# Turning normalised tokens in two 64-row halves of TensorE's array, each half of the tokens into its own PSUM bank

## The chip, the cores and the metric

The kernel runs on one core of one Trainium2 chip. The metric is the device time of one launch in microseconds. "Before" was timed in three runs; one more execution was profiled. TensorE (PE in the profile) multiplies out of SBUF into PSUM, which has eight banks of 512 fp32 per partition. VectorE is DVE, ScalarE is ACT, GpSimd is POOL, SyncE is SP and issues most DMAs.

## What is computed

One transformer block on a sequence of 4096 tokens of width 256, all in fp32: causal attention over normalised tokens, then a gated feed-forward part. Only the first lines of the attention matter here:

```python
mu = jnp.mean(x, axis=-1, keepdims=True)
var = jnp.mean(jnp.square(x - mu), axis=-1, keepdims=True)
xn = (x - mu) * jax.lax.rsqrt(var + LN_EPS) * gamma + beta
qkv = jnp.einsum('bne,fe->bnf', xn, w_qkv)
...
x = _layernorm(x + _L0_attn_ref(x, L0_attn_gamma, L0_attn_beta, L0_attn_w_qkv), axis=-1)
x = _layernorm(x + _L0_ffn_ref(x, ...), axis=-1)
```

The projection sums over the 256 features, so TensorE needs the features on partitions, while the statistics of a token are taken with tokens on partitions. Each chunk of normalised tokens is therefore turned once, and gamma and beta are applied on the way, where they are one number a partition.

## The kernel before

The tokens are cut in eight chunks of 512 (QB), each four tiles (TI) of 128 tokens. For a chunk c, VectorE takes mean and variance, ScalarE the root and VectorE the reciprocal. Then `normalise(c)` writes `xn_of(c)`, four tiles [128 tokens, 256 features] (VectorE for chunks 0 to 2, L806; POOL for 3 to 7, L609). `transpose_xn(c)` (L998) has TensorE turn them: for each half f of the features it takes one PSUM bank and makes four transposes of 128 tokens by 128 features (L1003), one beside the other, so that bank f holds [128 features, 512 tokens]. `copy_xnt(c)` (L679) has ScalarE copy each bank to `xnT` in one instruction of 512 columns with gamma as scale and beta as bias (L682). Everything that is projected (queries, keys, values) reads `xnT`.

The attention is made of a stream of operations that the class `Schedule` lays out once, in `PLAN.ops`; each engine walks through the same list and does its part. The kinds that matter: `norm` (turn and copy a chunk), `direct` (the first two blocks' queries and keys, L1024, copied by ScalarE in L674 and L676 and summed by POOL in L618), `qk` and `v` (projections, L1015 and L1040), `unit` (a 128-row tile of products whose row maxima VectorE takes, L1054 and L822/L825; for some of them ScalarE first copies one of the two banks to `mx_sb`, L711, and VectorE reduces that, L817), `score` (L1089 and L1094, two banks each; ScalarE takes the exponent in L728), `av` (product with the values, L1111), and `turn` (L1067 and L1075: turned sums and turned maxima, copied by ScalarE in L718 and L744). `norm` 0, 1 and 2 stand in the opening, `norm` 3 to 7 in the loop over blocks, each between the units of one step and an `av`.

Seven of the eight banks form a ring, `ring_bank(use)`. Which bank a use gets is planned by `take_banks`: it walks over the list with a small table of durations in nanoseconds (for a `norm`, 440 of TensorE and 730 of ScalarE for each bank) and gives each use the bank that its model has free first. `former[use]` is the use that had the bank before, and `ring_free(use)` makes TensorE wait for the engine that empties it. So these numbers do not move any instruction, but decide which bank an instruction writes and whom it waits for. Before, `ring_free` was called for bank f just ahead of its four transposes.

Engines signal by semaphores: `xn_done` (normalised tiles), `xnt_ready` (banks turned, one count per bank), `xnt_done` (copies made). TensorE waits for `xnt_done` ahead of the projections of that chunk. ScalarE works through its list strictly in order.

## Time and profile before

| | us |
|---|---|
| median of three runs | 2284.06 |
| lowest and highest run | 2283.5 and 2284.6 |
| profiled execution, its own time | 2284.38 |
| its span in the profile | 2282.8 |
| attention up to about | 1630 |
| feed-forward part from there to the end | 653 |

The page of a profile gives busy times of each engine over the span. PE is the matmul side of TensorE, PEld its weight loads. A timeline merges neighbouring instructions of one form into one row: its start, the length of the whole row, the engine, the line, the tiles and the count; in brackets stands how long the engine was idle ahead of it and who ended that. A group row gives the count, the busy time and the mean length of one, and the idle time ahead of such instructions. The granted TensorE clock is a share of full speed, 1.00 for 2.4 GHz and 0.50 for 1.2 GHz.

### The profile page before, as it was taken

To read this page: it belongs to the slowest core of one execution; us is meant where nothing else is said; L and a number is where in the kernel's file an instruction comes from. 1 tells how busy PE (TensorE), PEld (TensorE's weight loads), DVE (VectorE), ACT (ScalarE), POOL (GpSimd) and SP (SyncE) were. 2 spreads that over 40 slices of the span, in tenths; PEclk is the share of its full clock that TensorE was granted. 3 is DMA by queue.
4 is the path that set the end of the run, shared out by engine and by line. 5 is a ranking of instruction groups with operands and counts; after the bars stand their busy time and mean duration, and the time that the engine had idled before them with its cause. 6 is when DMAs were issued, how large, how long until landed. Compare 5 with 4: busy or idle time off the path is not lost. (4 is left out here: it accounts for less than half of the span.)

```text
span 2282.8 us, 40909 instructions
## 1 busy us (share of the span) xinstructions
PE 2253.1 (99%) x15594; PEld 1394.5 (61%) x15594; DVE 1738.5 (76%) x3748; ACT 1621.0 (71%) x3131; POOL 201.5 (9%) x237
## 2 busy tenths in 40 slices
PE   8999999999999999999999999999999999999998
PEld 5555555555555556555555555554588888888887
DVE  8899998888889897888989898996435445544543
ACT  4677888889999888889989899999723333432332
POOL 3211100011000102000010201001100000000000
PEclk9999999999999999999999999999999999999999
DMA  3110001100000200000020000205410000000000
GB/s 102 31 27 16 5 20 40 38 20 20 20 19 1 59 20 20 20 20 19 1 56 20 20 20 20 77 1 168 151 42 15 5 19 19 10 10 19 15 5 20
DMA packets 72295, 70.22 MB, mean 31 GB/s; under 512 B 41632, under 2 KB 51744, under 8 KB 70688
## 3 DMA queue, kind: packets, MB, share of 16 engines
q1 hardware_dynamic: 67392, 56.03, 9.3%
q0 software_dynamic: 4704, 11.53, 1.7%
q8 instruction: 124, 2.03, 0.4%
q14 instruction: 75, 0.61, 0.1%
HBM read 28.20 MB, written 4.19 MB: 14 GB/s over the span
## 5 line engine op out<-in xcount | busy, mean ns | idle before, releaser
L728 ACT ACTIVATE PR<-bank 128x512 f32<-128x512 f32 (+1 forms) x2176 | 1097.2, 593 | 75.6 <-PE bank L1094 70.6
L822 DVE TENSOR_REDUCE pm<-bank 128x1 f32<-128x512 f32 x1442 | 932.5, 684 | 134.2 <-PE bank L1054 114.9
L1111 PE MATMUL bank<-PR,V 128*17 128x512 f32 (+3 forms) x4608 | 553.2, 562 | 0.3 <-POOL PR L624 0.3
L1089 PE MATMUL bank<-MR,ones 64*128 64x512 f32 (+3 forms) x2304 | 464.7, 383 | 7.1 <-ACT sums L744 4.6
L1499 PE MATMUL bank<-e_hid,e_h_sb 128*128 128x512 f32 x2048 | 466.1, 389 | 0.0
L1499 PEld LDWEIGHTS bank<-e_hid,e_h_sb 128*128 128x128 f32 x2048 | 383.8, 188 | 81.1 <-DVE e_hid L1369 1.5
L1321 ACT ACTIVATE e_tmp<-bank,scales 128x512 f32<-128x512 f32 x128 | 88.3, 690 | 322.8 <-PE bank L1499 322.7
L1089 PEld LDWEIGHTS bank<-MR,ones 64*128 64x128 f32 x2304 | 239.6, 185 | 81.9 <-ACT PR L728 37.1
L825 DVE CUSTOM_DVE_ANT_0 bank<-bank,below 128x256 f32<-128x256 f32 (+3 forms) x512 | 239.9, 514 | 32.0 <-PE bank L1054 30.9
L711 ACT ACTIVATE mx_sb<-bank 128x512 f32<-128x512 f32 x350 | 209.8, 599 | 56.0 <-PE bank L1054 52.1
L1054 PEld LDWEIGHTS bank<-KA,QX 64*128 64x128 f32 x992 | 127.7, 183 | 186.7 <-ACT PR L728 76.9
L1054 PE MATMUL bank<-KA,QX 64*128 64x512 f32 (+3 forms) x992 | 237.5, 438 | 1.6 <-DVE pm L825 0.5
L817 DVE TENSOR_REDUCE pm<-mx_sb 128x1 f32<-128x512 f32 x350 | 236.8, 677 | 0.6
L1448 DVE CAST e_hid<-e_tmp 128x512 fp32r<-128x512 f32 x128 | 54.1, 423 | 237.4 <-ACT e_tmp L1321 237.4
L1094 PE MATMUL bank<-QX,KA 64*128 64x512 f32 x992 | 195.5, 379 | 0.0
L1054 PEld LDWEIGHTS bank<-KA,QA 64*128 64x128 f32 x736 | 95.3, 185 | 138.5 <-DVE pm L822 55.3
L1111 PEld LDWEIGHTS bank<-PR,V 128*17 128x17 f32 x4608 | 82.3, 95 | 150.9 <-issue 96.4
L1054 PE MATMUL bank<-KA,QA 64*128 64x512 f32 (+2 forms) x736 | 172.7, 434 | 1.6 <-DVE pm L822 0.2
L624 POOL TENSOR_SCALAR_AFFINE_SELECT PR<-PR 128x512 f32<-128x512 f32 (+1 forms) x96 | 78.7, 820 | 795.4 <-ACT PR L728 795.4
L1094 PE MATMUL bank<-QA,KA 64*128 64x512 f32 (+2 forms) x736 | 143.6, 375 | 0.0
L1369 DVE TENSOR_TENSOR e_hid<-e_tmp,e_hid 128x512 fp32r<-128x512 f32 x192 | 132.4, 689 | 5.3
L1481 PE MATMUL bank<-QX,KB 128*128 128x512 f32 x496 | 114.0, 389 | 1.7 <-PEq L331 1.7
(138 smaller groups left out, 1726.3 us busy)
## 6 DMA issues: line engine op xcount, KB each, us to landing
xnT<-in_h_dram SPq DMA_DIRECT2D x8, 1024.0 KB, 4.9
KA<-qk_hi SPq DMA_DIRECT2D x88, 64.0 KB, 2.2
KA<-qk_lo SPq DMA_DIRECT2D x88, 64.0 KB, 2.2
QX<-qk_hi SPq DMA_DIRECT2D x80, 64.0 KB, 2.2
QX<-qk_lo SPq DMA_DIRECT2D x80, 64.0 KB, 2.2
xres<-in_x_dram SPq DMA_DIRECT2D x8, 512.0 KB, 8.1
e_h_sb<-in_h_dram POOLq DMA_DIRECT2D x2, 2048.0 KB, 11.1
e_h_sb<-in_h_dram POOLq DMA_DIRECT2D x1, 4096.0 KB, 23.6
```

Source lines behind the costliest of these rows:

```text
L711: act.activation(mx_sb[:, k % NRB, :], ring_bank("unit", B, n, 0)[:, :], ACT.Copy).then_inc(mx_copied, 1)
L728: act.activation(PR[:, s % NPB, h, off:QB], ring_bank("score", s, h)[:, off:QB], ACT.Exp).then_inc(exp_done, 1)
L817: dve.reduce_max(pm[:, B % 2, i, a, p, 1 + c:2 + c], mx_sb[:, k % NRB, :], AX.X).then_inc(mx_done, 1)
L822: dve.reduce_max(pm[:, B % 2, i, a, p, 1 + c:2 + c], bank[:, :], AX.X).then_inc(mx_done, 1)
L825: dve.tensor_tensor_reduce(out=own, in0=own, in1=below[:, QB - P * (i + 1):QB], scale=1.0, scalar=-3.0e38, op0=ALU.add, op1=ALU.max, accum ...
L1054: pe.matmul(ring_bank("unit", B, n, a)[:, 0:width], q_slot(B)[rows(a), p, P * i:P * (i + 1)], k_slot(chunk_block(B, c))[rows(a), p, 0:widt ...
L1089: pe.matmul(ring_bank("score", s, h)[:, at:at + QB - q], ones[rows(a), p, :], MR[rows(a), B % NM, q:QB], start=True, stop=False)
L1094: done = pe.matmul(ring_bank("score", s, h)[:, at:at + QB - q], k_slot(chunk_block(B, tile // TI))[rows(a), p, keys], q_slot(B)[rows(a), p ...
L1111: last = pe.matmul(ACC[32 * h:32 * h + VW, q:QB], V[:, v_tile(B, tile), GH * (B // NJ % 2) + h, :], PR[:, s % NPB, h, at:at + QB - q], sta ...
L1369: dve.tensor_tensor(hid[:, buffer, 1, c, :], tmp[:, u % NTMP, :], hid[:, buffer, 0, c, :].bitcast(fp32), ALU.subtract).then_inc(parts_done, 1)
L1481: last = pe.matmul(RING[2 * (o % 3) + at][:, :], w[:, c, P * o:P * (o + 1)], x1T[:, part, c, :], start=(c == 0 and part == 0), stop=(c == ...
L1499: last = pe.matmul(RING[(4 + n) % NR][:, :], w[:, c, P * o:P * (o + 1)], hid[:, (T + layer) % 2, part, c, :], start=(c == 0 and part == 0) ...
```

## The change

TensorE turns a chunk in 16 transposes instead of eight. Each takes 64 tokens (half a of a tile's partitions, `rows(a)`) by 128 features, with the matching 64 by 64 block of the identity as the moving operand. The two halves alternate: half 0 writes bank 0 of the turn, half 1 bank 1. A bank then holds both halves of the features for the 256 tokens of one half: [feature half, tile, 64 tokens]. ScalarE empties a bank in two copies of 256 columns, one for each half of the features because gamma and beta differ, and each spreads its four pieces of 64 tokens over `xnT`. The last transpose of each half signals `xnt_ready` (still two counts a chunk); `xnt_done` now counts four a chunk, and all waits are rewritten for that. Both banks are taken, and waited for, ahead of the first transpose. In the planner a `norm` takes both banks at once, with 480 for TensorE and 900 for each bank's emptying by ScalarE.

```diff
-            if op[0] in ("norm", "x1_turn"):
+            if op[0] == "norm":
+                taken = [take(op + (a,)) for a in range(2)]
+                now += 480
+                for n in taken:
+                    by_scalar(n, now + 195, 900)
+            if op[0] == "x1_turn":
                 for f in range(EC):
                     n = take(op + (f,))
                     now += 440
...
             def normalise(c):
                 pool.wait_ge(rstd_done, 3)
-                pool.wait_ge(xnt_ready, EC * c)
+                pool.wait_ge(xnt_ready, 2 * c)
...
             def copy_xnt(c):
-                for f in range(EC):
-                    act.wait_ge(xnt_ready, EC * c + f + 1)
-                    act.activation(xnT[:, f, QB * c:QB * (c + 1)], ring_bank("norm", c, f)[:, :], ACT.Identity,
-                                   scale=gb[:, 0, f:f + 1], bias=gb[:, 1, f:f + 1]).then_inc(xnt_done, 1)
+                for a in range(2):
+                    act.wait_ge(xnt_ready, 2 * c + a + 1)
+                    turned = ring_bank("norm", c, a).rearrange("p (f i q) -> p f i q", f=EC, i=TI)
+                    for f in range(EC):
+                        tokens = xnT[:, f, QB * c:QB * (c + 1)].rearrange("p (i a q) -> p a i q", i=TI, a=2)
+                        act.activation(tokens[:, a, :, :], turned[:, f, :, :], ACT.Identity,
+                                       scale=gb[:, 0, f:f + 1], bias=gb[:, 1, f:f + 1]).then_inc(xnt_done, 1)
...
                 if former[0] == "norm":
-                    pe.wait_ge(xnt_done, EC * former[1] + former[2] + 1)
+                    pe.wait_ge(xnt_done, EC * (2 * former[1] + former[2] + 1))
...
             def transpose_xn(c):
+
                 pe.wait_ge(xn_done, TI * (c + 1))
+                for a in range(2):
+                    ring_free("norm", c, a)
                 for f in range(EC):
-                    ring_free("norm", c, f)
-                    for i in range(TI):
-                        last = pe.transpose(ring_bank("norm", c, f)[:, P * i:P * (i + 1)],
-                                            xn_of(c)[:, i, P * f:P * (f + 1)], ident[:, :])
-                    last.then_inc(xnt_ready, 1)
+                    for i in range(TI):
+                        for a in range(2):
+                            at = QB // EC * f + HALF * i
+                            last = pe.transpose(ring_bank("norm", c, a)[:, at:at + HALF],
+                                                xn_of(c)[rows(a), i, P * f:P * (f + 1)], ident[rows(a), rows(a)])
+                            if (f, i) == (EC - 1, TI - 1):
+                                last.then_inc(xnt_ready, 1)
...
             def project_direct(B, k):
                 p, side = divmod(k, 2)
-                pe.wait_ge(xnt_done, EC * (B + 1))
+                pe.wait_ge(xnt_done, 2 * EC * (B + 1))
```

The waits of `project_qk` and `project_v` are rewritten like that of `project_direct`. Line numbers of the changed program are 8 to 13 higher behind the edits: L1003 becomes L1015, L682 becomes L690, L1111 becomes L1124, L1054 becomes L1067.

No instruction changes its place against the others; what changes is the burst itself and its waits. On TensorE at chunk 5's turn, behind the units (L1054) and ahead of the product with the values (L1111; `xn` is the normalised chunk, `xn_done` its tiles, `exp_done` ScalarE's exponents, `mx_done` VectorE's reductions), there stood before

```order
L1054 MATMUL bank<-KA,QX 128x512 [waits mx_done]
L1003 MATMUL bank<-ident,xn 128x128 [waits exp_done,xn_done]
L1003 MATMUL bank<-ident,xn 128x128 x3
L1003 MATMUL bank<-ident,xn 128x128 [waits exp_done]
L1003 MATMUL bank<-ident,xn 128x128 x3
L1111 MATMUL bank<-PR,V 17x512 [waits exp_done]
```

and now

```order
L1067 MATMUL bank<-KA,QX 128x512 [waits mx_done]
L1015 MATMUL bank<-ident,xn 128x64 [waits exp_done,xn_done]
L1015 MATMUL bank<-ident,xn 128x64 x15
L1124 MATMUL bank<-PR,V 17x512 [waits exp_done]
L1124 MATMUL bank<-PR,V 17x512 x3
```

The second wait for an exponent, which stood behind four of the eight transposes, is joined to the one ahead of the first. On ScalarE at the same place, between the copies into `xnT` and the next step's copy of a unit (`mx_sb`) and exponents (`PR`), there stood before

```order
L728 ACTIVATE PR<-bank 128x512 [waits st_ready] x3
L682 ACTIVATE xnT<-bank,gb 128x512 [waits xnt_ready] x2
L711 ACTIVATE mx_sb<-bank 128x512 [waits mx_done,mx_ready]
L728 ACTIVATE PR<-bank 128x512 [waits st_ready,av_done]
L728 ACTIVATE PR<-bank 128x512 [waits st_ready] x3
```

and now

```order
L736 ACTIVATE PR<-bank 128x512 [waits st_ready] x3
L690 ACTIVATE xnT<-bank,gb 128x4x64 [waits xnt_ready]
L690 ACTIVATE xnT<-bank,gb 128x4x64
L690 ACTIVATE xnT<-bank,gb 128x4x64 [waits xnt_ready]
L690 ACTIVATE xnT<-bank,gb 128x4x64
L719 ACTIVATE mx_sb<-bank 128x512 [waits mx_done,mx_ready]
```

Two copies have become four, ahead of the same `mx_sb` copy. Behind the turn of chunk 3 the planner now hands out other banks. On TensorE the next unit behind `turn` 1 wrote and waited for, before,

```order
L1054 MATMUL bank5<-KA,QX 128x128 [waits xnt_done]
L1054 MATMUL bank6<-KA,QX 128x128 [waits mx_done]
L1054 MATMUL bank2<-KA,QX 128x512 [waits mx_done]
L1054 MATMUL bank0<-KA,QX 128x512 [waits xnt_done]
L1089 MATMUL bank3<-MR,ones 128x256 [waits mx_done]
```

and now

```order
L1067 MATMUL bank6<-KA,QX 128x128 [waits mx_done]
L1067 MATMUL bank5<-KA,QX 128x128 [waits xnt_done]
L1067 MATMUL bank2<-KA,QX 128x512 [waits mx_done]
L1067 MATMUL bank3<-KA,QX 128x512 [waits mx_done]
L1102 MATMUL bank0<-MR,ones 128x256 [waits xnt_done]
```

The units have given the banks that `xnT`'s copies free to later users. Of 4,624 uses of a ring bank in the whole plan, 57 follow another use than before; most of the others only carry another bank's number.

## Rows read from the trace of the kernel before

**Rows 1.** The page: busy us, share of the span, instructions of each engine

```profile
PE 2253.1 (99%) x15594; PEld 1394.5 (61%) x15594; DVE 1738.5 (76%) x3748; ACT 1621.0 (71%) x3131; POOL 201.5 (9%) x237
```

**Rows 2.** Groups by form: out<-in, xcount | busy us, mean ns | idle us before, its end

```profile
L682 ACT ACTIVATE xnT<-bank,gb 128x512 f32<-128x512 f32 x16 | 11.7, 788 | 4.2 <-PE bank L1003 4.2
...
L711 ACT ACTIVATE mx_sb<-bank 128x512 f32<-128x512 f32 x350 | 209.8, 599 | 56.0 <-PE bank L1054 52.1
...
L718 ACT ACTIVATE MR<-bank 128x256 fp32r<-128x256 f32 x64 | 21.1, 382 | 19.0 <-PE bank L1075 19.0
...
L1003 PE MATMUL bank<-ident,xn 128*128 128x128 f32 x48 | 6.4, 277 | 0.4 <-POOL xn L609 0.2
```

**Rows 3.** Timeline near 88 us, TensorE: start us, length us, what, count, [idle before]

```profile
87.70 0.46 PE L1067 MATMUL bank<-ident,acc_sb 64*128 64x64 f32 x8
...
87.97 0.61 PE L1075 MATMUL bank<-ident_r,mneg 64*128 64x64 f32 x8
```

**Rows 4.** Timeline of the opening, TensorE

```profile
10.99 1.04 PE L1003 MATMUL bank<-ident,xn 128*128 128x128 f32 x8
...
13.22 3.67 PE L1024 MATMUL bank<-xnT,PR 128*128 128x512 f32 x8 [1.19 <-ACT xnT L682]
...
16.73 1.04 PE L1003 MATMUL bank<-ident,PR 128*128 128x128 f32 x8
...
17.60 3.60 PE L1024 MATMUL bank<-xnT,PR 128*128 128x512 f32 x8
```

**Rows 5.** Timeline of the opening, ScalarE

```profile
11.62 1.45 ACT L682 ACTIVATE xnT<-bank,gb 128x512 f32<-128x512 f32 x2 [3.60 <-PE bank L1003]
...
21.23 0.69 ACT L674 ACTIVATE qk_lo<-bank,sign 128x512 fp32r<-128x512 f32 x1 [0.45 <-PE bank L1024]
...
33.45 0.69 ACT L674 ACTIVATE qk_lo<-bank,sign 128x512 fp32r<-128x512 f32 x1 [0.66 <-PE bank L1024]
```

**Rows 6.** Timeline around chunk 3's turn

```profile
53.71 2.14 ACT L728 ACTIVATE PR<-bank 128x512 f32<-128x512 f32 x4 [2.43 <-PE bank L1094]
...
55.73 1.09 PE L1003 MATMUL bank<-ident,xn 128*128 128x128 f32 x8
...
56.42 1.45 ACT L682 ACTIVATE xnT<-bank,gb 128x512 f32<-128x512 f32 x2 [0.57 <-PE bank L1003]
...
58.61 0.66 ACT L718 ACTIVATE MR<-bank 128x256 fp32r<-128x256 f32 x2 [0.75 <-PE bank L1075]
```

**Rows 7.** Timeline around chunk 4's turn

```profile
96.38 1.09 PE L1003 MATMUL bank<-ident,xn 128*128 128x128 f32 x8 [0.25 <-POOL xn L609]
...
97.07 1.45 ACT L682 ACTIVATE xnT<-bank,gb 128x512 f32<-128x512 f32 x2
...
98.92 0.60 ACT L711 ACTIVATE mx_sb<-bank 128x512 f32<-128x512 f32 x1 [0.40 <-PE bank L1054]
...
98.95 0.69 DVE L822 TENSOR_REDUCE pm<-bank 128x1 f32<-128x512 f32 x1 [0.85 <-PE bank L1054]
```

**Rows 8.** Timeline around chunk 5's turn

```profile
145.61 2.07 ACT L728 ACTIVATE PR<-bank 128x512 f32<-128x512 f32 x4
...
146.84 1.06 PE L1003 MATMUL bank<-ident,xn 128*128 128x128 f32 x8
...
147.53 1.47 ACT L682 ACTIVATE xnT<-bank,gb 128x512 f32<-128x512 f32 x2
...
149.35 0.60 ACT L711 ACTIVATE mx_sb<-bank 128x512 f32<-128x512 f32 x1 [0.34 <-PE bank L1054]
```

**Rows 9.** Timeline behind chunk 6's turn, ScalarE

```profile
212.06 0.64 ACT L711 ACTIVATE mx_sb<-bank 128x512 f32<-128x512 f32 x1
```

**Rows 10.** Timeline behind chunk 7's turn, ScalarE

```profile
285.38 0.60 ACT L711 ACTIVATE mx_sb<-bank 128x512 f32<-128x512 f32 x1 [0.34 <-PE bank L1054]
```

**Rows 11.** Window 48:50 (PE, PEld, DVE, ACT, POOL busy; clock; DMA), and timeline at 47 us

```profile
48.00:50.00 2.00, 2.00 (x11) 2.00 (x11) 1.44 (x6) 0.00 (x0) 1.35 (x2) 0.50 0.02 4
...
47.15 3.12 PE L1040 MATMUL bank<-wvg,xnT 128*128 128x128 f32 x13
```

4 lines of the change are left out of this document (2 added, 2 removed).

## The prediction, made before the changed kernel was run

> **What bounds the kernel now.** I read four views, from coarse to fine. The page first: TensorE counts as busy 99% of the span, VectorE 76%, ScalarE 71% [rows 1]. That TensorE share is no proof of a bound, since matmul ends are modelled and a matmul that waits inside a burst looks busy; what matters is whom it waits for at each place. Only the attention stage (up to about 1630 us) is touched. The feed-forward stage behind it neither reads `xnT` nor uses the banks' plan, so it only moves as a whole.
>
> Then the groups by form, for the two kinds of instruction that change. The copy of turned tokens into `xnT` (L682) is 16 instructions of 512 columns at 788 ns [rows 2]. The turning itself (L1003) is eight bursts of eight matmuls; 48 of the 64 stand in one row, the 16 of chunks 1 and 2 read another buffer and have the same length. So the change touches 11.7 us of ScalarE's time and eight bursts of about 1.05 us on TensorE. Even if all of it were on the path, it is half a per cent; most is not.
>
> Then the timeline at the eight turns: chunks 0, 1 and 2 at 11, 17 and 28 us in the opening, chunks 3 to 7 at 56, 96, 147, 210 and 283 us in the loop. The reader is to see in each who sits idle behind it. In the opening ScalarE was idle 3.60 us before chunk 0's copies, and TensorE was idle 1.19 us after them: that turn is on the path [rows 4, 5]. After chunk 1's copies ScalarE still waits 0.45 us for TensorE, and before the last direct product's copy 0.66 us [rows 5]. In the loop ScalarE reaches the next copy (L711) with only 0.40 us idle after chunk 4, 0.34 us after chunks 5 and 7, and none after chunk 6 [rows 7 to 10]. These small gaps are the only cover for longer copies.
>
> **TensorE's part.** It now issues 16 transposes of 64 tokens with 64 moving columns instead of 8 of 128. The nearest row is exact in form: the transposes of `acc_sb` (L1067), 64 rows by 64 columns, alternating between the two halves of the array and two banks. Eight take 0.46 us by their modelled ends, and the next burst starts 0.27 us after the first of them [rows 3]. One lasts 222 ns, so they start (0.46 - 0.22) / 7 = 0.034 us apart. Sixteen then occupy 16 x 0.034 = 0.54 us. Today's burst occupies 17.60 - 16.73 = 0.87 us [rows 4]. TensorE saves 0.33 us a chunk, 2.6 us in eight.
>
> The tokens are ready later, though. Both banks are now filled by the last pair: 15 x 0.034 + 0.22 = 0.73 us after the start. Before, ScalarE began when the first bank was full, 11.62 - 10.99 = 0.63 us after the start in chunk 0 and 56.42 - 55.73 = 0.69 us in chunk 3 [rows 4 to 6], which is 3 x 0.11 + 0.27 = 0.60 us plus 0.03 to 0.09 for the signal. With 0.06 for the signal the copies can begin 0.79 us after the start, 0.13 us later than today.
>
> **ScalarE's part.** Four copies of 256 columns instead of two of 512. No row has this form with scale and bias. The nearest two: a plain copy of 512 columns (L711) takes 599 ns, one of 256 columns in the same pattern of four pieces (L718) 382 ns [rows 2]. The 256 columns less are worth 0.217 us, so the new copy should last 0.788 - 0.217 = 0.57 us. Two copies take 1.45 us today [rows 5], so they start 0.66 us apart; the new ones 0.66 - 0.22 = 0.44 us apart. Four: 3 x 0.44 + 0.57 = 1.90 us, which is 0.45 us more a chunk. Bounds: at the pace of L718, without the cost of scale and bias, 4 x 0.38 = 1.53 us at most (+0.1); without any overlap 4 x 0.57 = 2.28 us (+0.8). I take +0.45, since both terms of it come from the same kind of copy.
>
> **The wait for two banks.** The second bank's release used to be waited for after four transposes, 4 x 0.11 = 0.44 us into the burst; now both are waited for ahead of the first. Where it frees late, the burst starts late. In chunk 5 the two banks come from the second and third exponent of one step. The four exponents take 2.07 us at 0.60 each, so they start 0.49 us apart, and the third ends at 145.61 + 0.98 + 0.60 = 147.19 us. The burst started at 146.84 us, right after the second [rows 8]. It would now start near 147.29 us, 0.45 us later, which eats the 0.33 us saved, and the copies could begin at 147.29 + 0.79 = 148.08 us instead of 147.53: 0.55 us later, behind idle time of ScalarE. In chunk 3 they are the third and fourth exponent; the fourth ends at 55.85 us, so the burst slips from 55.73 to about 55.95 us [rows 6]. In chunks 4, 6 and 7 the second bank is one that VectorE or ScalarE gives back earlier. POOL's next normalising waits on the same signals (now two per chunk), which come long before it needs them; the queues of SP are not moved.
>
> **The sum for the opening.** Chunk 0: copies end 0.13 + 0.45 = 0.58 us later, and TensorE's first direct product with them. TensorE gains 0.33 us at chunk 1 (shift 0.25) and again at chunk 2 (shift about -0.08). ScalarE is 0.58 + 0.45 = 1.03 us late after chunk 1 but had 0.45 us of idle before the copy at 21.23 us [rows 5] and TensorE's own start 0.25 us late ahead of it; the 0.3 us left are only the second of POOL's sums for chunk 0, which TensorE needs a whole projection later. After chunk 2 it is 0.25 + 0.45 = 0.70 us late against the 0.66 us idle at 33.45 us [rows 5]. So what enters the loop is -0.1 to +0.1 us: zero.
>
> **The sum for the loop.** Chunk 3: the slip of 0.22 us, 0.13 for readiness and 0.45 of copies, 0.80 us in all, lies against 0.75 us of idle before the next copy [rows 6]: zero. Chunk 4: the copies start at 96.38 + 0.79 = 97.17 us instead of 97.07, 0.10 + 0.45 - 0.40 = 0.15 us late [rows 7]. Chunk 5: 0.55 + 0.45 - 0.34 = 0.66 us [rows 8]. Chunk 6: ScalarE has work until the copies anyhow, and no idle behind them: 0.45 us [rows 9]. Chunk 7: 0.10 + 0.45 - 0.34 = 0.21 us, taking its start as chunk 4's [rows 10]. Together 1.5 us. Each is ScalarE's lateness at a copy that VectorE's next reduction and the next four exponents stand behind, and I let it stand in full, though a later step may win some back. TensorE's 0.33 us in these chunks meets the same late banks and counts nothing.
>
> The profiled execution took 2284.38 us (span 2282.8 and 1.58 around it); with the sum 2285.9. It lies 0.3 us above the median of 2284.06, so against the median I forecast **2285.6 us**. A difference of 0.2% (4.6 us), about what a measurement of this kernel can tell from no change, is not in the forecast.
>
> **Rivals.**
> (a) *TensorE's saving arrives.* VectorE sits idle 0.85 us behind chunk 4's burst, waiting for TensorE [rows 7]; if that is the chain, 8 x 0.33 = 2.6 us go away and the copies are hidden: 2284.1 - 2.6 = 2281.4. Against it: chunk 5 loses its saving to the bank. Chance 0.13.
> (b) *The halves do not overlap, so the change does not do what it says.* At today's pace of 0.109 us for 128 columns [rows 4], 16 x 0.054 = 0.87 us: nothing saved, and the copies ready 15 x 0.054 + 0.22 + 0.06 = 1.09 us after the start, 0.30 later than I reckon. The opening then enters the loop 0.9 us late, and chunks 4, 5 and 7 add 0.3 each: 2285.6 + 1.8 = 2287.4. The burst of L1067 speaks against it, but it is eight long and had stood queued. Chance 0.10. The Trainium skill's page "TensorE: Matmul & The Clock Gate" (Back-to-back issue gap) has a rule of this kind: with hardware decode off a matmul costs the sequencer about 62 ns, however few its columns. An estimate by it is 16 x 0.062 = 0.99 us a burst and 2288 us in all; the 0.034 us of rows 3 disagrees with it.
> (c) *Other banks, other waits.* The planner prices the turns anew, and 57 of 4,624 uses of a bank follow another use than before, in five places behind chunks 3 to 7 (and at the very end). A swapped wait can cost or give back about one copy or reduction, 0.60 us [rows 2], a place: 5 x 0.6 = 3 us either way, 2282.6 to 2288.6. Chance 0.12.
> (d) *The half clock lasts longer or shorter.* Between 42 and 50 us TensorE ran at 0.50 of its clock (1.2 GHz) and 13 matmuls of the values took 3.12 us [rows 11]; at the full clock it would be half. A shift of tenths of a microsecond could move the end of this stretch across them: 1.6 us either way about the forecast, 2284.0 or 2287.2. Chance 0.08.
> (e) *Slower: ScalarE is the bound at all eight turns.* Then no idle covers anything: 8 x 0.45 = 3.6 us of copies, and later starts of 0.13 us at chunk 0, 0.35 at chunk 3, 0.10 at chunks 4 and 7 and 0.55 at chunk 5, together 4.8 us: 2288.9. It decides from the point where the idle of 0.34 to 0.75 us behind the copies is not slack but is needed further on. ScalarE's 71% speaks against it. Chance 0.07.
> The forecast holds 0.50.
>
> **How the numbers follow.** The range runs from (a) to (b) with the near side of (c), 2281.3 to 2287.8; it leaves out (e) and the outer ends of (c) and of the copies' bounds (+0.8 in place of +0.45 would add 0.35 in four chunks, 1.4 us). Faster by over 0.2% needs less than 2279.5 us, for which I have no mechanism beyond (a) and (c) together: 0.03. Slower by over 0.2% means more than 2288.6 us: (e), and a little of (c): 0.09. Within 0.2%: 0.88.
>
> **What would show it.** The transposes: median length of 0.22 us, 16 in about 0.73 us; 0.9 us or more is (b). The copies: 0.57 us each, four in 1.9 us. Chunk 5's burst starting some 0.45 us later against the exponents ahead of it. The second product of values starting within 0.1 us of 47.15 us shows that the opening cancels. L711 behind chunks 4 to 7 later against its neighbours by 0.15, 0.66, 0.45 and 0.21 us, with no idle ahead of it. The start of the feed-forward stage later by the whole difference. I am wrong if that start moves by more than 3 us, or if the feed-forward stage changes length.

## The result, and the profile after

| | before | after |
|---|---|---|
| median of 22 runs each, us | 2284.15 | 2288.8 |
| lowest and highest run | 2283.5 and 2285.88 | 2287.17 and 2290.23 |
| span of the profiled execution | 2282.8 | 2287.9 |

The change makes the kernel slower: ratio 1.002, 95% interval 1.0014 to 1.0025, some 4.6 us. The forecast was 2285.6 us, so its direction held and its size did not: 1.5 us were forecast, 4.6 came, and 2288.8 lies outside the range of 2281.3 to 2287.8.

First the page of the changed kernel (busy us, share of the span, count), which answers to [rows 1], and its row for the DMA queue that brings instruction code (packets, MB, share of 16 engines):

```profile
span 2287.9 us, 41053 instructions
...
PE 2254.9 (99%) x15658; PEld 1394.2 (61%) x15658; DVE 1738.3 (76%) x3748; ACT 1624.2 (71%) x3147; POOL 201.0 (9%) x237
...
q8 instruction: 124, 2.03, 0.4%
```

TensorE has 64 matmuls and 64 weight loads more than before (15,658 against 15,594), 128 instructions. The prediction priced their array time and never their number. The groups by form answer to [rows 2]: the copies, the neighbouring plain copy, and the transposes of chunks 3 to 7 and 0.

```profile
L690 ACT ACTIVATE xnT<-bank,gb 128x256 f32<-128x256 f32 x32 | 15.5, 570 | 4.2 <-PE bank L1015 3.9
...
L719 ACT ACTIVATE mx_sb<-bank 128x512 f32<-128x512 f32 x350 | 209.4, 598 | 55.1 <-PE bank L1067 51.1
...
L1015 PE MATMUL bank<-ident,xn 64*128 64x64 f32 x96 | 4.3, 227 | 1.4 <-ACT PR L736 0.7 <-DVE pm L833 0.3 <-POOL xn L614 0.3
```

Copies of 570 ns and transposes of 227 ns are what was forecast (0.57 and 0.22 us). So the instructions themselves hold no surprise, and the missing 3 us are elsewhere.

To find them I compared when the same work starts in both traces: ScalarE's exponents (L728 before, L736 after), one after the other, each less its start in the trace of before. Such a curve shows at which place a kernel falls behind. The column is the time before at that place, all in us:

```
place               60    91   121   150   216   288   386   567   775  1036  1150  1179  1627
after             1.14  1.83  2.14  2.62  3.12  2.88  3.43  2.70  3.82  3.94  4.22  5.02  4.99
before, repeated  -0.2 to -0.4 throughout
```

Four parts stand out. 1.14 us are there at 60 us, and 0.69 more by 91 us. The turns of chunks 4 to 6 add 1.3 us up to 216 us, about as forecast. And then there are three steps of 2.5 us together far behind the last turn (chunk 7, at 286 us), where nothing that was changed runs any more: between 288 and 386, 567 and 775, and 1150 and 1179 us. Smaller changes stand between them, -0.6 us in sum, the largest a gain of 0.7 us between 386 and 567 us; so 1.1 + 0.7 + 1.3 + 2.5 - 0.6 give the 5.0 us of this trace. The feed-forward stage has the same length and only moves: its first row of L1494, which began at 1635.96 us, begins 4.98 us later.

```profile
1640.94 2.32 PE L1494 MATMUL bank<-QX,KB 128*128 128x512 f32 x9 [1.67 <-PEq L336]
```

What happens at the step near 763 us shows in the queue of SP, which issues the DMAs that stack a projected chunk (`qk_hi`, `qk_lo`) into `QX` and `KA`. First before, then after: start, length of the row, two issues each.

```profile
759.39 1.23 SPq L531 DMA_DIRECT2D KA<-qk_hi  x2
760.65 1.23 SPq L531 DMA_DIRECT2D QX<-qk_hi  x2
761.92 1.23 SPq L531 DMA_DIRECT2D KA<-qk_hi  x2
```

```profile
762.02 1.23 SPq L536 DMA_DIRECT2D KA<-qk_hi  x2
763.29 2.44 SPq L536 DMA_DIRECT2D QX<-qk_hi  x2
765.77 1.23 SPq L536 DMA_DIRECT2D KA<-qk_hi  x2
```

The same two issues take 2.44 us instead of 1.23. The round of stacking behind them has its projection copied by ScalarE into `qk_hi`, which must wait until the round before has been read. That copy before, at this place and at the place near 1163 us, and then in after at the same two places:

```profile
764.90 0.69 ACT L692 ACTIVATE qk_hi<-bank,qscale 128x512 fp32r<-128x512 f32 x1 [0.94 <-DMA KA<-qk_hi]
...
1162.16 0.69 ACT L692 ACTIVATE qk_hi<-bank,qscale 128x512 fp32r<-128x512 f32 x1 [0.93 <-DMA KA<-qk_hi]
```

```profile
768.75 0.69 ACT L700 ACTIVATE qk_hi<-bank,qscale 128x512 fp32r<-128x512 f32 x1 [2.15 <-DMA KA<-qk_hi]
...
1167.16 0.69 ACT L700 ACTIVATE qk_hi<-bank,qscale 128x512 fp32r<-128x512 f32 x1 [1.72 <-DMA KA<-qk_hi]
```

ScalarE waits 2.15 us instead of 0.94 at the first and 1.72 instead of 0.93 at the second. In after, a packet of the instruction queue starts at 763.1 and one at 1164.7 us, and the long single issues (1.80 and 1.57 us, where others take 0.6) start at 763.3 and 1164.7 us. In before, the packet that belongs here starts at 771.4 us and the long issue at 771.5 (1.30 us), in a round behind which the next copy into `qk_hi` comes only 12 us later, at 783.85 us, with no wait for a DMA. The step at 386 us is of the same kind: in after a packet starts at 379.5 us, an issue of 1.49 us at 379.7, and ScalarE waits 1.83 us for the stacking of `KB`, where before it waited 1.09 us for the projection. At 1164 us the long issue itself is not what ScalarE waits for. It waits for the round's DMAs from `qk_hi`, and the long one, from `qk_lo`, stands behind the last of them. In after:

```profile
1163.39 1.23 SPq L536 DMA_DIRECT2D KA<-qk_hi  x2
1164.67 2.20 SPq L536 DMA_DIRECT2D QA<-qk_lo  x2
```

That last DMA from `qk_hi` takes 3.0 us from issue to landing, in the row of the DMA view. It takes 3.1 to 3.5 us in four other traces with this step (both repeats, the old plan, before with the fill in front), and 2.2 to 2.3 us in before and in two traces without it (both fills, after with the fill behind).

```profile
KA<-qk_hi SPq DMA_DIRECT2D x1, 64.0 KB, 3.0
```

So at such a packet DMAs under way land later too, and not only the next issue takes longer. At 763 us the DMAs that ScalarE waits for are issued behind the long issue and land in the usual 2.2 us; there it is the issue.

The DMA queues between 760 and 766 us, before and then after (whose stacking starts later in this window); the packet of queue 8 is only in the second:

```profile
q1 hardware_dynamic: 464, 0.65, 44.0%
```

```profile
q1 hardware_dynamic: 219, 0.32, 21.8%
q8 instruction: 1, 0.02, 1.7%
q14 instruction: 1, 0.01, 0.5%
```

The long issues go with these packets everywhere. Of SP's 483 DMA issues between 60 and 1630 us, 14 to 17 in each trace take more than 0.9 us (0.9 to 2.2, median 1.4). In all 17 traces together these are 270, and for 269 of them a packet of queue 8 starts between 0.55 us before and 0.2 us after the issue starts, while a trace has some 97 such packets in that stretch. The other way round, 249 packets start while SP issues one DMA right behind another, and 244 of them meet a long issue.

The 124 packets of that queue bring 2.03 MB, 16.4 KB each, one every 18 us on average. The theory from here: code comes in blocks of a fixed count of instructions, 128 more of them shift every later block against the program, and some blocks now come while DMAs that ScalarE waits for are issued or under way.

### The profile page after: what moved, and what is told of

Its sections match the earlier page's. It is cut to its first block and busy times, and to the rows that moved or that the text cites. A ratio compares the mean times of both kernels' runs of the same rounds, so it can differ in the third digit from the quotient of the medians.

```text
span 2287.9 us, 41053 instructions
## 1 busy us (share of the span) xinstructions
PE 2254.9 (99%) x15658; PEld 1394.2 (61%) x15658; DVE 1738.3 (76%) x3748; ACT 1624.2 (71%) x3147; POOL 201.0 (9%) x237
## 3 DMA queue, kind: packets, MB, share of 16 engines
q8 instruction: 124, 2.03, 0.4%
## 5 line engine op out<-in xcount | busy, mean ns | idle before, releaser
L736 ACT ACTIVATE PR<-bank 128x512 f32<-128x512 f32 (+1 forms) x2176 | 1096.7, 595 | 75.1 <-PE bank L1107 70.5
L1124 PE MATMUL bank<-PR,V 128*17 128x512 f32 (+3 forms) x4608 | 553.2, 562 | 0.3 <-POOL PR L629 0.3
L719 ACT ACTIVATE mx_sb<-bank 128x512 f32<-128x512 f32 x350 | 209.4, 598 | 55.1 <-PE bank L1067 51.1
L1067 PEld LDWEIGHTS bank<-KA,QX 64*128 64x128 f32 x992 | 128.9, 184 | 189.9 <-ACT PR L736 75.0
L1067 PE MATMUL bank<-KA,QX 64*128 64x512 f32 (+3 forms) x992 | 240.3, 440 | 2.8 <-ACT qk_sb L702 0.7
L1067 PEld LDWEIGHTS bank<-KA,QA 64*128 64x128 f32 x736 | 95.2, 185 | 138.7 <-DVE pm L830 54.8
L1067 PE MATMUL bank<-KA,QA 64*128 64x512 f32 (+2 forms) x736 | 172.9, 434 | 1.6 <-DVE pm L830 0.2
L1124 PEld LDWEIGHTS bank<-PR,V 128*17 128x17 f32 x4608 | 82.2, 95 | 150.4 <-issue 96.0
L1494 PE MATMUL bank<-QX,KB 128*128 128x512 f32 x496 | 114.0, 390 | 1.7 <-PEq L336 1.7
```

Source lines behind the costliest of these rows:

```text
L719: act.activation(mx_sb[:, k % NRB, :], ring_bank("unit", B, n, 0)[:, :], ACT.Copy).then_inc(mx_copied, 1)
L736: act.activation(PR[:, s % NPB, h, off:QB], ring_bank("score", s, h)[:, off:QB], ACT.Exp).then_inc(exp_done, 1)
L1067: pe.matmul(ring_bank("unit", B, n, a)[:, 0:width], q_slot(B)[rows(a), p, P * i:P * (i + 1)], k_slot(chunk_block(B, c))[rows(a), p, 0:widt ...
L1124: last = pe.matmul(ACC[32 * h:32 * h + VW, q:QB], V[:, v_tile(B, tile), GH * (B // NJ % 2) + h, :], PR[:, s % NPB, h, at:at + QB - q], sta ...
L1494: last = pe.matmul(RING[2 * (o % 3) + at][:, :], w[:, c, P * o:P * (o + 1)], x1T[:, part, c, :], start=(c == 0 and part == 0), stop=(c == ...
```

## The experiments

The theories, as I name them here: **bound** (rival (e), ScalarE's longer copies are on the path at every turn), **banks** (rival (c), the planner's new numbers), **clock** (the half clock that after shows at 14 us), and **code** (the count of TensorE's instructions). Each kernel was timed in turn with before; "added" counts TensorE instructions against before. "Steps" is the sum of the three differences of the curve named above, "at 60" and "end" the curve at 60 and 1627 us.

The 95% interval of such a ratio is some 2 us wide to either side, 3 us for the two with increments. The medians of five kernels lie within it: copies in two pieces, opening only, fill behind, two copies and both fills, 0.14 to 1.63 us above before. For them speaks that the medians of before itself differ by 0.3 us at most, and that their curves agree. One trace is one execution: "after, fill in front" was traced in the fastest of its eleven runs (2285.07 us), so its curve, 1.11 us at the end, doesn't explain its median.

| kernel | added | median | less before | at 60 | steps | end |
|---|---|---|---|---|---|---|
| after | 128 | 2288.8 | 4.65 | 1.14 | 2.47 | 4.99 |
| after, repeated | 128 | 2288.48 | 4.06 | 1.14 | 2.02 | 4.47 |
| after, repeated again | 128 | 2288.57 | 4.15 | 0.98 | 2.45 | 3.96 |
| before, repeated | 0 | 2284.37 | -0.05 | -0.19 | -0.08 | -0.29 |
| before, copies in two pieces | 0 | 2284.98 | 0.56 | 0.39 | 0.00 | 0.52 |
| after, 128 increments | 256 | 2295.28 | 10.94 | 10.06 | -0.03 | 10.68 |
| before, 128 increments | 128 | 2296.47 | 12.13 | 9.42 | 2.54 | 12.90 |
| after, old plan | 128 | 2288.76 | 4.42 | 0.59 | 2.85 | 4.23 |
| opening only | 48 | 2285.14 | 0.80 | 1.07 | 0.07 | 0.77 |
| after, fill in front | 256 | 2287.26 | 2.92 | -0.14 | -0.07 | 1.11 |
| before, fill in front | 128 | 2286.73 | 2.39 | 0.38 | 2.07 | 2.53 |
| after, fill behind | 256 | 2285.97 | 1.63 | 0.09 | 0.11 | 1.99 |
| one half first, fill in front | 256 | 2285.73 | 1.39 | 0.28 | 0.04 | 0.98 |
| two copies, fill behind | 256 | 2284.52 | 0.14 | 0.66 | -0.12 | 0.55 |
| before, both fills | 256 | 2285.20 | 0.82 | 0.49 | -0.01 | 0.53 |
| one half first, fill behind | 256 | 2286.93 | 2.55 | 2.06 | -0.08 | 2.07 |

**After, repeated.** Is what one trace shows there in a second one?

> The changed kernel again. Its trace shows TensorE at 0.50 of its clock in the opening (the first direct products took 5.37 us against 3.67 before), exponents 1.2 us late at 42 us, about 3.0 us late at 289 us and 5.0 us late at the end of the attention stage. If the half clock in the opening is a matter of where the execution happens to lie, this second trace may lack it and the timed runs scatter by more than the 1.2 us of before; if the change always causes it, it is there again. If the 1.1 us lost at 763 us (a DMA issue of SP that took 1.8 us instead of 0.59 while TensorE's code was being loaded) belongs to the code's length, it stands at the same issue again; if it is chance, elsewhere.

2288.48 us (2287.57 to 2290.3, 11 runs), 4.06 above before (2284.42). The same steps at the same places, so they belong to the program.

**Empty instructions.** 64 ahead of TensorE's first matmul and 64 among the units of block 1, in after and in before.

```diff
+            for _ in range(64):
+                pe.nop(nofuse=True)
...
+                    if op[1] == 1 and 6 <= op[2] < 14:
+                        for _ in range(8):
+                            pe.nop(nofuse=True)
```

> The changed kernel with 128 empty instructions on TensorE, 64 ahead of its first wait (idle to 4.0 us) and 64 ahead of units of block 1 (where VectorE sets the pace). The change added 128 instructions to TensorE (64 matmuls, 64 weight loads); code arrives in blocks of about 256 (124 loads for some 31,500 instructions), so with 128 more every later block boundary lies at the same program place as in the kernel before. Theory that the boundaries cost 2 us behind 300 us: 1.5 to 2.5 us faster than the changed kernel, 2286.5 or so, and the 1.1 us at block 15's stacking gone. Theory that only ScalarE's copies and the clock cost time: no faster, 2288.8 plus whatever the empty instructions cost.

> The kernel before with the same 128 empty instructions on TensorE, nothing else. Theory of the code's block boundaries: they now lie where the changed kernel has them, 1.5 to 2.5 us slower than before, 2286. Rival: 2284.2 plus at most 0.5 us that the empty instructions themselves cost.

2288.57 and 2284.37 us. These say nothing on the code: the pages count 41,053 and 40,909 instructions, as without the edit, so the empty instructions aren't in the programs. I read both as repeats. As such they serve twice. They give the scatter of a curve: 0.2 to 0.4 us between two traces of before, while three of after end between 3.96 and 4.99 us. And they give a trace of after in which TensorE keeps its full clock at 14 us and which still ends 4.0 us late. That goes against **clock** as the main cause.

**Before, each bank copied in two pieces.** ScalarE's longer copies alone.

```diff
-                    act.activation(xnT[:, f, QB * c:QB * (c + 1)], ring_bank("norm", c, f)[:, :], ...)
+                    for half in range(2):
+                        to = slice(QB * c + QB // 2 * half, QB * c + QB // 2 * (half + 1))
+                        last = act.activation(xnT[:, f, to], ring_bank("norm", c, f)[:, ...], ...)
+                    last.then_inc(xnt_done, 1)
```

> The kernel before with each turned bank copied in two pieces of 256 tokens instead of one of 512: ScalarE's part of the change alone, with TensorE's transposes, banks and code as before. My sum's terms put the copies at 0.45 us a chunk: about +0.5 in the opening, 0.1 to 0.45 at chunks 4 to 7, together 1.5 us: 2285.7. Theory that ScalarE bounds all eight turns: 3.6 us, 2287.8. Theory that the copies are covered: 2284.2.

2284.98 us (2284.46 to 2285.34): 0.56 above before, against 4.65 for the change. ScalarE does all the extra copying here, so **bound** falls as the main cause. It is also less than the 1.5 us that my own terms gave. The curve adds 0.27, 0.01 and 0.39 us at chunks 4, 5 and 6, where after has 0.31, 0.48 and 0.50. With the old transposes, whose first bank is ready early, four copies cost less than they do in after (below).

**128 more TensorE instructions that stay in the program.** Increments of a semaphore that nobody waits for, at the same places as the empty ones.

```diff
+        pad_sem = sem("pad_sem")
...
+            for _ in range(64):
+                pe.sem_inc(pad_sem, 1)
...
+                            pe.sem_inc(pad_sem, 1)
```

> The changed kernel with 128 semaphore increments on TensorE that nobody waits for, 64 ahead of its first wait and 64 ahead of units of block 1. Two more traces of the changed kernel lose time at the same places behind 300 us: about 0.4 us at 383, 0.8 to 1.2 at 767 and 0.8 to 1.3 at 1166 us, where ScalarE waits 2.2 instead of 0.9 us for the stacking DMAs, while a load of TensorE's code stands at the same moment as one long DMA issue of SP. With 128 more instructions a boundary of the code's blocks of 256 lies at each program place where it lay before. Theory: those three losses go, 2286.3 us (2288.5 less 2.4, plus up to 0.5 for the increments). Rival (the losses come from something else): 2288.5 or more.

> The kernel before with the same 128 semaphore increments on TensorE and nothing else. Theory of the code's blocks: the boundaries now lie where the changed kernel has them, and the losses at 383, 767 and 1166 us appear: 2286.5 to 2287. Rival: 2284.4 plus up to 0.5 for the increments themselves.

2295.28 us (2294.71 to 2297.44, 5 runs) and 2296.47 us (2294.59 to 2298.37, 5 runs), before at 2284.34. The increments in front are dear, which I had not expected: TensorE's first matmul starts at 10.91 us instead of 4.0. The row is of after with the increments:

```profile
10.91 6.48 PE L1005 MATMUL bank<-below,ident 128*128 128x512 f32 x10 [10.91 <-issue]
```

So the totals can't be compared with before, but the curves can from 60 us on. Before with 128 more goes from 9.42 to 12.90 and has the steps of after (2.54 us in three), although its turns are untouched; the other 0.9 us comes between 60 and 68 us, at a stretch of half clock (below). After with 128 more goes from 10.06 to 10.68 and has none, and is the faster of the two. A theory that looks at the turns alone can't give this order; **code** gives it, with one thing added: another 128 cancel the first 128. What counts is where the blocks begin, and that repeats with 256 instructions; a page has one packet of code more where 256 were added. 16.4 KB for 256 makes 64 bytes each, an estimate.

**The planner's old numbers**, and **the new manner for chunks 0 to 2 alone.** Both from one source that has both manners; `PRICED` says which turns the planner prices anew, `NEW` which are done anew.

```diff
-            if op[0] == "norm":
+            if op[0] == "norm" and op[1] in PRICED:
...
+PRICED = ()
+NEW = (0, 1, 2, 3, 4, 5, 6, 7)
```

The second has `(0, 1, 2)` in both.

> The changed kernel with the planner's old numbers for a turn (440 and 730, one bank after the other), so that the ring's banks are handed out as before. If the 57 changed predecessors cost time it is faster than 2288.5 by up to 1.5 us; if they cost nothing it stays within 0.3 us of 2288.5, with the losses at chunks 5 and 6 and at 383, 767 and 1166 us as they were.

> Chunks 0 to 2 turned in the new manner, 3 to 7 in the old (copies, banks and planner's numbers each as their manner has them). TensorE has 48 instructions more than before, not 128. The opening's share of the loss is about 1.0 us at 60 us in the traces, 0.4 of it also there with the copies alone. Theory: 2285.3 if the code's blocks with 48 more fall harmlessly, up to 2287 if they do not. If the whole loss sat in the opening (clock and copies): 2288.5.

2288.76 us (2288.23 to 2289.78) with the old plan, as after has: **banks** falls. 2285.14 us (2284.4 to 2286.71) for the opening alone: by the medians its price is 0.8 us, not the zero of the prediction. It adds 48 instructions, and there are no steps.

**64 small transposes of the identity in front**, into banks that nothing uses yet, in after and in before. They are 128 TensorE instructions, cheaper than the increments.

```diff
+            def fill():
+                for n in range(32):
+                    for a in range(2):
+                        pe.transpose(banks[5 + a][:, HALF * (n % 8):HALF * (n % 8 + 1)], ident[rows(a), :],
+                                     ident[rows(a), rows(a)])
+            fill()
```

> The changed kernel with 64 small transposes of the identity (128 instructions of TensorE) in the time in which TensorE waits for VectorE's constants before 4.0 us. The pace of the changed bursts (0.034 us each) makes them 2.2 us, so they should cost at most 0.3 us. Theory of the code's blocks: the losses at 383, 767 and 1166 us go, 2.2 to 2.5 us in the traces, and the timed runs come to 2286.3. Rival: 2288.5 or more.

> The kernel before with the same 64 small transposes at the start and nothing else. Theory of the code's blocks: 2.5 us slower than before without any change in the work of the attention, 2286.9, with steps of about 0.35, 1.1 and 1.1 us at 383, 767 and 1166 us. Rival: 2284.4 to 2284.7.

The two cross, as with the increments, and now in the median: before gets slower by 2.39 us (2286.73, 2285.66 to 2288.63), and after gets faster by more than a microsecond (2287.26, 2285.07 to 2288.51) though it does more. That is less than the 2.2 us and more that I expected of it, and why its runs scatter by 3.4 us I don't know. Before with the fill, SP's queue and ScalarE's copy near 763 us:

```profile
761.51 2.06 SPq L531 DMA_DIRECT2D QX<-qk_hi  x2
```

```profile
766.60 0.69 ACT L692 ACTIVATE qk_hi<-bank,qscale 128x512 fp32r<-128x512 f32 x1 [1.77 <-DMA KA<-qk_hi]
```

The long issue and the long wait of after stand here in a kernel whose turns are those of before, and a packet of the instruction queue starts at 762.0 us. The fill isn't free in front: it takes 3.68 us at the start, and TensorE's own first work begins 1.7 us later.

**The fill behind chunk 0's turn** in after, where TensorE idles 2.1 us for ScalarE's copies.

```diff
                     transpose_xn(op[1])
+                    if op[1] == 0:
+                        fill()
```

> The changed kernel with the same 64 small transposes put behind chunk 0's turn, where TensorE waits 2.1 us for ScalarE's copies. In two of its four traces the clock was at 0.50 from 13.8 to 17.2 us, behind that idle time, in none of four traces with the transposes of before. If the idle time lets the clock fall and filling it keeps it up: no stretch at 0.50 before 38 us and narrower runs, 2285.8 to 2286.3 with the code's blocks realigned. If small transposes do not keep it up: as the one with the fill at the start.

2285.97 us (2285.41 to 2286.43), 1.63 above before where after lies 4.06 to 4.65 above: 2.4 to 3.0 us faster, with 64 transposes added. No steps; ScalarE's wait near 763 us is 0.9 us again. Its runs lie within 1.0 us, those of after within 3.1.

**One half first, then the other** (fill in front): all eight transposes of half 0 and then those of half 1, each behind its own bank.

```diff
-                for f in range(EC):
-                    for i in range(TI):
-                        for a in range(2):
+                for a in range(2):
+                    ring_free("norm", c, a)
+                    for f in range(EC):
+                        for i in range(TI):
```

> As the fill at the start, but the eight transposes of half 0 run first and then those of half 1, each bank waited for ahead of its own eight, so nothing overlaps in the array and the second bank is needed later. If the halves overlap, a burst takes longer here (0.87 us and more instead of 0.54), but the first bank is ready after eight, and chunk 5's step of 0.5 us (its burst waits for the third exponent) should go. If overlap is worth nothing on the path: 0.3 to 0.8 us faster than the fill at the start; if it is worth what I forecast: slower.

2285.73 us, with a wide scatter (2284.96 to 2289.37), so the medians of this and of the kernel with the fill in front are no sure difference. The runs fall into two groups by TensorE's mean granted clock: six at 0.997 take 2284.96 to 2285.73 us, five at 0.995 or 0.996 take 2287.75 to 2289.37; the trace is of the first. The trace answers two questions of the prediction. Its burst at chunk 5 and the copies behind it:

```profile
148.03 1.10 PE L1014 MATMUL bank<-ident,xn 64*128 64x64 f32 x16
...
148.75 1.48 ACT L690 ACTIVATE xnT<-bank,gb 128x256 f32<-128x256 f32 x3
```

Sixteen transposes take 1.10 us instead of 0.71 when they don't alternate, so alternating halves do overlap. And the loss at chunk 5 (0.48 us of the curve in after, 121 to 150 us) is 0.07 here: without the wait for two banks it goes. It takes the four copies too, as the next experiment shows.

**One copy for each bank** (fill behind): 512 columns with the first feature half's gamma and beta for both halves. The second half's gamma and beta are left out, so that two copies of 512 columns stand in for four of 256.

```diff
-                    for f in range(EC):
-                        tokens = xnT[:, f, QB * c:QB * (c + 1)].rearrange("p (i a q) -> p a i q", i=TI, a=2)
-                        act.activation(tokens[:, a, :, :], turned[:, f, :, :], ACT.Identity, ...)
+                    tokens = xnT[:, :, QB * c:QB * (c + 1)].rearrange("p f (i a q) -> p a f i q", i=TI, a=2)
+                    act.activation(tokens[:, a, :, :, :], turned[:, :, :, :], ACT.Identity, ...)
```

> As the fill behind chunk 0's turn (2285.97), but ScalarE empties each bank in one copy of 512 columns, with the first feature half's gamma and beta for both halves: the second half's own gamma and beta are left out. TensorE's part of the change alone, code blocks realigned. The split copies by themselves cost 0.6 us in the kernel before. If the two parts add up: 2285.4, with chunk 5's step of 0.5 us still there and chunks 4 and 6 without theirs. If TensorE's saving of 0.33 us a chunk were worth its full sum once the copies are short: below 2284.

**Both fills in before**, 256 instructions more and nothing else.

> The kernel before with 64 small transposes at the start and 64 behind chunk 0's turn: 256 instructions of TensorE more, one whole block of its code. With 128 more it took 2286.7. Theory of the blocks' position: the steps at 383, 767 and 1166 us are gone, and only what the second fill costs remains, since it takes 2.2 us where TensorE was idle 1.2 us: 2284.4 plus 0.2 to 1.2. Rival (each added instruction costs, or the code's sheer length): 2288 to 2289, twice the loss of 128.

Two copies: 2284.52 us (2283.9 to 2285.22), 0.14 above before (2284.38), and not the 2285.4 of the expectation. So with the blocks back in place and without the two extra copies a turn, the new transposes cost and gain nothing that can be measured. The split of the copies is worth 1.63 - 0.14 = 1.5 us. I had expected chunk 5 to keep its step of 0.5 us; it adds 0.13. The rows there show why:

```profile
148.57 0.72 PE L1014 MATMUL bank<-ident,xn 64*128 64x64 f32 x16 [0.46 <-ACT PR L735]
```

```profile
149.35 1.45 ACT L689 ACTIVATE xnT<-bank,gb 128x512 f32<-128x512 f32 x2 [0.43 <-PE bank L1014]
150.73 0.60 ACT L718 ACTIVATE mx_sb<-bank 128x512 f32<-128x512 f32 x1
```

The burst is as late as in after, and the copies start 0.43 us after ScalarE ran out of work, but ScalarE had 0.34 us of idle time behind them in before [rows 8] and that covers nearly all of it. The late start alone costs next to nothing, the longer copies alone cost next to nothing there (0.01 us), and both together 0.48. Before with 256 more: 2285.2 us (2284.36 to 2286.2), and a curve that is 0.49 at 60 us and stays there; 128 instructions cost 2.1 us in steps, 256 none. Its rows at the place, with the issue and the wait of before:

```profile
761.23 1.23 SPq L531 DMA_DIRECT2D QX<-qk_hi  x2
```

```profile
765.48 0.69 ACT L692 ACTIVATE qk_hi<-bank,qscale 128x512 fp32r<-128x512 f32 x1 [0.95 <-DMA KA<-qk_hi]
```

Its page counts 125 packets of code, one more than before.

**A kernel to beat both**: one half first, with the fill behind chunk 0's turn.

> The new transposes with one half after the other, each bank waited for ahead of its own eight, and the 64 small transposes behind chunk 0's turn: both known losses beside the split copies taken away. 2285.97 less chunk 5's 0.5 us: 2285.5. If it came under 2284.2 the new manner would beat the old; by the sum it does not, since the split copies' 0.6 us stay and the saving on TensorE is not on the path.

2286.93 us (2285.89 to 2287.64), 2.55 above before and slower than with alternating halves. It is already 2.06 us late at 60 us. I put that down to the bursts of 1.1 us in the opening, but it isn't shown: the kernel with the same bursts and the fill in front is 0.28 us late there. No version of this turn beat the kernel before.

## Why the prediction was wrong

What became of the 4.65 us: about 2.4 from the position of the code, which the steps measure best (2.0 to 2.5 us in three traces of after, 2.1 in before with the fill in front). Two differences of medians lie near that but hold something else as well: the 2.39 us of before with the fill in front have 0.4 us from the opening in them, and the 2.4 to 3.0 us by which the fill behind makes after faster have what it gives back in the opening. Then about 1.5 us from four copies instead of two, given the new bursts; about 0.1 from the transposes; and half a microsecond left, in the opening and its clock. The last three are differences of medians within their intervals and are estimates. Now by the prediction's own steps.

**TensorE's part: right.** The bursts of after at chunks 4 and 5, with ScalarE's copies and what stands behind them, which answer to [rows 7, 8]:

```profile
98.27 0.71 PE L1015 MATMUL bank<-ident,xn 64*128 64x64 f32 x16 [0.32 <-POOL xn L614]
...
98.99 1.93 ACT L690 ACTIVATE xnT<-bank,gb 128x256 f32<-128x256 f32 x4
...
100.81 0.61 ACT L719 ACTIVATE mx_sb<-bank 128x512 f32<-128x512 f32 x1
```

```profile
147.76 2.07 ACT L736 ACTIVATE PR<-bank 128x512 f32<-128x512 f32 x4
...
149.48 0.71 PE L1015 MATMUL bank<-ident,xn 64*128 64x64 f32 x16 [0.47 <-ACT PR L736]
...
150.20 1.93 ACT L690 ACTIVATE xnT<-bank,gb 128x256 f32<-128x256 f32 x4 [0.37 <-PE bank L1015]
...
152.01 0.61 ACT L719 ACTIVATE mx_sb<-bank 128x512 f32<-128x512 f32 x1
...
152.65 0.69 DVE L825 TENSOR_REDUCE pm<-mx_sb 128x1 f32<-128x512 f32 x1 [0.29 <-ACT mx_sb L719]
```

0.71 us a burst against 0.73 forecast, starts (0.71 - 0.23) / 15 = 0.032 us apart; the copies begin 0.72 us after the burst, 0.79 forecast. Rival (b) is refuted. The Trainium skill's page "TensorE: Matmul & The Clock Gate" (Back-to-back issue gap) gives some 62 ns a matmul for the case that hardware decode is off, by which a burst would be near 1 us; at 0.032 us apart and 0.71 us a burst this trace shows that this floor doesn't bind here.

**ScalarE's part: right** in the length, 1.93 us against 1.90 forecast.

**The wait for two banks: right.** The burst at chunk 5 starts 149.48 - 147.76 = 1.72 us behind the first exponent of its step, instead of 1.23 [rows 8], 0.49 later against 0.45 forecast, and the release is now the exponents (L736). At chunk 3 ScalarE's wait for the burst grew from 0.57 [rows 6] to 0.86 us.

**The sum for the loop: right in all, roughly.** By the curve chunks 4, 5 and 6 add 0.31, 0.48 and 0.50 us, against 0.15, 0.66 and 0.45 forecast, and the idle ahead of the next copy (L719) is gone as foretold: 0.40 and 0.34 us stood there [rows 7, 8]. The form of chunk 5's term (late start and longer copies, less that idle time) also fits where one of the two is taken away: 0.07 us without the wait, 0.13 without the longer copies. Chunk 7 adds nothing (0.21 forecast): the curve even falls by 0.24. Chunk 3 was taken as zero, and behind it the curve rises by 0.69 us between 60 and 68 us; that is the clock's, below.

**The sum for the opening: the first step that failed, a term mis-sized.** I let TensorE's 0.33 us a turn pay the 0.58 us of chunk 0. The repeat of after that keeps its clock is the clean case:

```profile
10.88 0.71 PE L1015 MATMUL bank<-ident,xn 64*128 64x64 f32 x16
...
13.70 3.67 PE L1037 MATMUL bank<-xnT,PR 128*128 128x512 f32 x8 [2.11 <-ACT xnT L690]
...
17.30 0.71 PE L1015 MATMUL bank<-ident,PR 64*128 64x64 f32 x16
17.95 3.70 PE L1037 MATMUL bank<-xnT,PR 128*128 128x512 f32 x8
```

Against [rows 4]: from chunk 0's burst to the first product it is 2.82 us instead of 2.23, 0.59 more, as forecast (0.58). Chunk 1's burst gives back (17.60 - 16.73) - (17.95 - 17.30) = 0.22 us, not 0.33, and the two rows of products eat 0.2 of it again (3.60 instead of 3.51 us to the next burst, 3.70 instead of 3.60 us long). So 0.56 us are left where I had 0.25, and the third turn doesn't give them back: the old plan has 0.59 at 60 us, the repeat 0.98. The medians say 0.8 (opening only).

**Rival (d), the half clock: not the one stretch I named, but another.** In after the stretch at 47 us is still there, 41.1 to 51.3 us at 0.50 (1.2 GHz) against 40.0 to 50.2 before. A new one stands from 13.8 to 17.2 us. The opening of after, where [rows 4] had products of 3.67 us at the full clock:

```profile
9.93 0.72 PE L1015 MATMUL bank<-ident,xn 64*128 64x64 f32 x16
...
12.76 5.37 PE L1037 MATMUL bank<-xnT,PR 128*128 128x512 f32 x8 [2.11 <-ACT xnT L690]
...
18.06 0.71 PE L1015 MATMUL bank<-ident,PR 64*128 64x64 f32 x16
```

And the window (length; busy us of PE, PEld, DVE, ACT, POOL; granted clock; DMA share and GB/s):

```profile
14.00:17.00 3.00, 3.00 (x5) 1.01 (x4) 3.00 (x10) 1.26 (x2) 0.13 (x1) 0.50 1.07 340
```

The eight products take 5.37 us, 1.70 more than at the full clock. TensorE had stood idle for 2.11 us before; in before it was 1.19. I saw this in three of the traces with the new opening (after, its first repeat, opening only), in which chunk 0's burst began at 9.89 to 9.94 us; in those where it began at 10.47 and 10.88 us it did not come, and the 60 us mark is passed 0.1 to 0.6 us earlier. So the price is mostly that an early start is lost. The clock explains some of the 3.1 us over which after's runs scatter: six of the 22 have a mean granted clock of 0.995 or 0.996 and take 2289.22 to 2290.23 us, five have 0.998 and take 2287.43 to 2288.62. Which of the stretches makes the difference isn't shown. The fill in the gap has no stretch at 14 us and its runs scatter by 1.0 us, but those of the old plan, which has the gap and no fill, scatter by 1.6.

The other new stretch lies from 61.6 to 65.0 us, behind chunk 3's turn, where before and the second repeat of after ran at 1.00. The window in after:

```profile
62.00:65.00 3.00, 3.00 (x17) 2.58 (x15) 2.26 (x7) 1.87 (x6) 0.68 (x1) 0.50 0.00 0
```

All six traces of the new manner with a stretch near 61 us lose 0.6 to 1.1 us between the marks of 60 and 68 us, and the four without it (second repeat, old plan, opening only, one half first with the fill behind) 0.02 at most. After with the increments has one long stretch from 49.0 to 62.6 us instead and is left out. It isn't the new manner's own: before with the increments has such a stretch from 70.3 to 73.7 us, at the same place of a program that runs 9.4 us late, and loses 0.9 us there. This is a real cost of those executions, 0.7 us in the profiled one, and half of (d)'s mechanism: a new stretch, of a size within its 1.6 us. What makes it come or not was not tested.

**Rivals (a), (c) and (e).** (a) fell: no run gained from TensorE's 0.33 us. (c) fell by the run with the old plan. (e) had foretold 2288.9 us, almost the measured value, by a wrong cause: 3.6 us of copies and 1.2 us of later starts. Copies in four pieces cost 0.56 us in before and 1.5 us in after, and with the code's position put right after is at 2285.97, not at 2288.9. A total that fits is no proof of a mechanism.

**The step that failed above all** is a term that the prediction puts at nothing without a reason: I had every instruction's duration and asked of none what its being there does. The loop behind 286 us was taken for granted, since nothing changed runs there; but every block of TensorE's code behind the first turns now begins at another place of the program, and that stretch lost 2.0 to 2.5 us in three steps. The prediction's own test, "I am wrong if that start moves by more than 3 us", caught it: 4.98.

**What stays open.** That the position of TensorE's code costs 2.4 us is shown, by kernels that add instructions and nothing else. In all sixteen traces the three steps sum to 2.0 to 2.9 us where 128 instructions are added, and to -0.12 to 0.11 where none, 48 or 256 are. That the load of a block itself holds up SP's issue, and the DMAs under way, is read from the times of its packet and the long issue, which go together in 269 of 270 cases and move together when instructions are added; no experiment moved the one without the other, so that both follow from something third isn't excluded. Why the first step (at 386 us) is only 0.2 and 0.3 us in two of the traces, why all kernels with changed copies into `xnT` gain 0.7 us between 386 and 567 us and lose 0.3 between 1036 and 1150, and what scatters the runs of before and of after with the fill in front by 3.0 and 3.4 us, I could not explain.

## What to carry to other kernels

Count the instructions a change adds to each engine, not only their time: in a long unrolled program they shift every later block of code against the work, and here that was worth 2.4 us, more than all that the forecast had counted. To measure such a change fairly, pad both versions so that the blocks lie alike (here a multiple of 256 on TensorE), and look for time lost where nothing was changed. A shorter burst on an engine gains nothing if its consumer needs all of it before it may start: here 0.33 us a turn were forecast to be saved, and 0.45 us of copies came in at every turn and 0.45 us of a second bank's wait at one of them.

## What was unexpected of the hardware

- A DMA issue on SP takes 0.6 us, but 0.9 to 2.2 us where a packet of TensorE's instruction code starts at the same time (244 of 249 packets that start within a row of issues, all traces together). DMAs under way then land in 3.0 us instead of 2.2 at 1164 us. At the two places where ScalarE waits for such a round of stacking near 763 and 1164 us that cost 1.2 and 0.8 us of wait.
- 64 semaphore increments ahead of TensorE's first matmul moved it from 4.0 to 10.91 us, 0.11 us each; 64 transposes of 64 columns, which are 128 instructions, moved it by 1.7 us at the start and took 2.19 us at the full clock behind chunk 0's turn.
- Alternating between the array's two 64-row halves, transposes start 0.032 us apart; sixteen in the order of one half first, then the other, take 1.01 to 1.10 us instead of 0.71.
- Idle time of 2.1 us on TensorE in the opening was followed by the half clock (0.50, 1.2 GHz) in three traces and not in two others of the same opening. With 64 transposes of no use in the gap the stretch didn't come, in a trace whose first burst began at 9.98 us, near the 9.89 to 9.94 us of the three.
- TensorE can get its full clock after nothing but small transposes. In before with both fills the two halves' transposes start as a pair each 0.107 us from 2.11 us on; at 5.39 us the full clock is granted, and the last pairs come 0.07 us apart, before any other matmul has run.
